# One 128-partition load with a zero-stride source in place of two 64-partition loads, in an attention block with two feed-forward layers

## What is computed

```python
h = _layernorm(x, axis=-1) * (1 + ca) + sa
q = (h @ Wq) -> (b, 16, l, 64);  k, v = (h @ Wk), (h @ Wv) -> (b, 4, l, 64), repeated 4 times
q = q * cos + _rotate_half(q) * sin        # k too
attn = einsum('bhqd,bhkd->bhqk', q, k) / 8 + slopes * rel
out = einsum('bhqk,bhkd->bhqd', softmax(attn), v) @ Wo
x = x + ga * out
```

## Time and profile before

| | us |
|---|---|
| median of 3 runs | 1219.91 (1217.07 to 1220.34) |
| profiled execution | 1218.02 |
| its span, first to last instruction | 1216.2 |
| PE / DVE / POOL / ACT busy | 1091.9 / 902.6 / 685.9 / 638.2 |
| DMA | 89.02 MB, mean 73 GB/s |
| stage one | 0 to about 120 |
| 32 heads | about 120 to 740 |

### The profile page before, as it was taken

The page is one execution under the profiler, slowest core; times in us unless marked ns, Lnnn a source line. Parts: engine busy times, 40 slices in busy tenths (PEclk is TensorE's granted clock), DMA queues, the critical chain, the costliest instruction groups (busy, mean ns, idle before and its releaser), DMA issues. The chain is left out here.

```text
span 1216.2 us, 23070 instructions
## 1 busy us (share of the span) xinstructions
PE 1091.9 (90%) x8352; PEld 666.1 (55%) x8352; DVE 902.6 (74%) x1584; ACT 638.2 (52%) x1000; POOL 685.9 (56%) x478
## 2 busy tenths in 40 slices
PE   5873799999999999999999999578899898999988
PEld 3552354554455545454544547446566795666678
DVE  6984776777777777777677744699998589888767
ACT  2442265656656665556565652145555555555554
POOL 3662156666667566665666665475555337555516
PEclk9996699999999999999999999789999999999999
DMA  8799412514325143152421100201111100111111
GB/s 245 252 246 341 103 39 59 113 37 100 72 49 114 38 107 71 41 114 50 101 71 36 45 19 26 72 18 29 31 24 37 25 2 18 30 30 31 31 26 34
DMA packets 83455, 89.02 MB, mean 73 GB/s; under 512 B 32740, under 2 KB 66064, under 8 KB 83344
## 3 DMA queue, kind: packets, MB, share of 16 engines
q1 hardware_dynamic: 83344, 87.55, 28.5%
HBM read 53.57 MB, written 24.25 MB: 64 GB/s over the span
## 5 line engine op out<-in xcount | busy, mean ns | idle before, releaser
L823 DVE CUSTOM_DVE_ANT_0 junk<-psum,alibi 128x1024 bf16<-128x1024 f32 x256 | 312.9, 1222 | 165.6 <-PE psum L888 158.3
L795 ACT ACTIVATE E<-psum,keybias_sb 128x1024 f32<-128x1024 f32 x256 | 274.8, 1112 | 190.2 <-PE psum L912 176.9
L732 POOL TENSOR_TENSOR xpos_sb<-xpos_sb,E 128x1024 f32<-128x1024 f32 x96 | 231.1, 2408 | 138.7 <-ACT E L795 134.3
L924 PE MATMUL psum<-E,V 128*64 128x512 f32 x1024 | 247.9, 605 | 0.0
L888 PE MATMUL psum<-KH,QH 64*128 64x512 f32 x512 | 121.2, 469 | 25.2 <-DVE M L823 20.0
L924 PEld LDWEIGHTS psum<-E,V 128*64 128x64 f32 x1024 | 62.1, 136 | 117.7 <-issue 111.7
L888 PEld LDWEIGHTS psum<-KH,QH 64*128 64x128 f32 x512 | 49.7, 190 | 119.2 <-DVE M L823 104.5
L736 POOL TENSOR_TENSOR xpos_sb<-xpos_sb 128x1024 f32<-128x1024 f32 x32 | 76.0, 2375 | 69.0 <-DVE xpos_sb L833 69.0
L912 PE MATMUL psum<-QH,KH 64*128 64x512 f32 x512 | 102.4, 396 | 0.7 <-DVE M L823 0.7
L912 PE MATMUL psum<-QL,KH 64*128 64x512 f32 x512 | 101.6, 392 | 0.0
L912 PE MATMUL psum<-QH,KL 64*128 64x512 f32 x512 | 101.5, 392 | 0.0
(11 more groups left out here) (145 smaller groups left out, 2143.8 us busy)
## 6 DMA issues: line engine op xcount, KB each, us to landing
QH<-qa_scratch SPq DMA_DIRECT2D x64, 256.0 KB, 4.7
qa_scratch<-tH SPq DMA_DIRECT2D x8, 1024.0 KB, 5.1
qa_scratch<-tL SPq DMA_DIRECT2D x8, 1024.0 KB, 7.4
QL<-qa_scratch SPq DMA_DIRECT2D x64, 128.0 KB, 4.8
XF<-inverse_scratch SPq DMA_DIRECT2D x32, 256.0 KB, 3.5
vp_att<-v_att SPq DMA_DIRECT2D x64, 128.0 KB, 2.3
KH<-k_scratch SPq DMA_DIRECT2D x16, 256.0 KB, 3.9
KL<-k_scratch SPq DMA_DIRECT2D x16, 256.0 KB, 5.1
```

The lines of the kernel that those rows point to most:

```text
L732: pool.tensor_tensor(sum_p[:, s, :], first, E[:, k % 4, :], ALU.add)\
L795: act.activation(E[:, k % 4, :], scores(k % 2), ACT.Exp, bias=kb).then_inc(exp_done, 1)
L823: dve.tensor_tensor_reduce(junk[:, :], banks(max_bank(i, k), 2), alibi[:, s, :], -1.0, BIG, ALU.add, ALU.min, M[:, s, k:k + 1]).then_inc(m ...
L924: last = pe.matmul(banks(6 + i % 2)[HD * ch:HD * ch + HD, :], V[:, g, k, :], E[:, k % 4, ch * 512:(ch + 1) * 512], start=(k == 0), stop=(k ...
```

## The change

The two transfers that fill the two halves of a tile become one over 128 partitions. Its source pattern has a leading dimension of 2: with stride zero for `QH`, `KH`, `KL` (the same 64 rows twice), with a stride of half a row for `QL`. The transfers of `V` stay. The counts that PE waits for follow: two transfers for queries instead of four, three for keys and values instead of five.

```diff
+        def twice(rows):
+
+            return rows[None].to_broadcast([2, HD, TB, P])
+
         def load_qa(sp, i, s):
             high, low = parts_of(qa_d, i // H, i % H)
-            for ch in range(2):
-                rows, half = slice(HD * ch, HD * ch + HD), slice(TB // 2 * ch, TB // 2 * (ch + 1))
-                sp.dma_start(QH[rows, s, :].bitcast(F32).rearrange("p (t c) -> p t c", c=P), high)\
-                    .then_inc(ld_qa[s], 16)
-                sp.dma_start(QL[rows, s, :].bitcast(F32).rearrange("p (t c) -> p t c", c=P), low[:, half])\
-                    .then_inc(ld_qa[s], 16)
+            sp.dma_start(QH[:, s, :].bitcast(F32), twice(high)).then_inc(ld_qa[s], 16)
+            sp.dma_start(QL[:, s, :].bitcast(F32), low.rearrange("p (a t) c -> a p (t c)", a=2)).then_inc(ld_qa[s], 16)
 
         def load_kv(sp, g, s):
             high, low = parts_of(k_d, g // KV, g % KV)
-            for dst, src in ((KH[0:HD], high), (KH[HD:P], high), (KL[0:HD], low), (KL[HD:P], low)):
-                sp.dma_start(dst[:, s, :].bitcast(F32).rearrange("p (t c) -> p t c", c=P), src)\
-                    .then_inc(ld_kv[s], 16)
+            for dst, src in ((KH, high), (KL, low)):
+                sp.dma_start(dst[:, s, :].bitcast(F32), twice(src)).then_inc(ld_kv[s], 16)
             sp.dma_start(V[:, s, :, :], v_d[g // KV, :, :, g % KV * HD:(g % KV + 1) * HD]).then_inc(ld_kv[s], 16)
...
-                            need(pe, ld_qa[s], 64 * (i // 4 + 1))
+                            need(pe, ld_qa[s], 32 * (i // 4 + 1))
                             if i % GROUP == 0:
-                                need(pe, ld_kv[g], 80 * (i // (2 * GROUP) + 1))
+                                need(pe, ld_kv[g], 48 * (i // (2 * GROUP) + 1))
```

## The result

The kernel with the change takes **1502.12 us** (median of 6 runs, 1498.96 to 1503.41) against 1219.54 (6 runs, 1217.07 to 1220.34): a ratio of 1.232 with an interval of 1.2301 to 1.2337. The profiled execution took 1502.15, its span is 1500.4. The forecast was 1445 with a range of 1400 to 1640: the sign and the mechanism are the forecast's, the time is 57 us above it. In the changed kernel the lines from L165 on are one lower than before (L912 is L911, L839 is L838), and the queries' loads are L164 and L165.

The account below looks back on a forecast made before the run. PE bounds the attention heads, DMA the first stage's loads and stores. Terms of +47.3 (first stage), +148.8 (groups), +12.7 (head 0), +2.4 (other heads) and +16 (clock) sum to 227 on 1218: 1445 us, range 1400 to 1640.

Parts of the forecast that it names:

- Two engines: Each merged load, its source led by 2, runs on two of 16 DMA engines, always the same two; chance 0.84.
- Rival 1: Merged loads use all 16 engines and both halves: up to 8.5 us faster, 1209.5 us; chance 0.08.
- rival 2: Merged loads use all 16 engines at today's rate: no change, 1218 to 1220 us; chance 0.03.
- rival 3: Merged loads run on two engines at 14.0 GB/s each: 2004 us; chance 0.05.
- QH's time to landing: Sign on the queries' load: its landing time rises from 4.7 to about 11 us or more.
- The price of a byte: Each of the two engines moves 26.9 GB/s, so a head's QH and QL take 14.6 us.
- First stage: Loads of three heads and one group take 63.3 us plus 1.0 for V instead of 17: +47.3 us.
- There is no cover left: In the first stage pair 4's stores queue behind the loads; ACT, DVE and PE, already 15.59 us late, wait for them.
- Ordinary heads: Heads without a new group turn from PE-bound to just DMA-bound: 19.2 us against 18.6, +0.6 each.
- closed loop: In heads, QH's issue through QM, den, reciprocal, inverse store and XF to the next QH: 19.2 us.
- Heads with a group: Heads loading new keys and values take 41.6 us; each of six groups costs +24.8 us, together +148.8.
- Clock: After PE idles in group heads, restarts run partly at 1.2 GHz: 2 to 3 us each, seven times, +16 us.

Follow-up runs that it names:

- leading 16: The changed kernel with its 128-partition loads read by a source pattern of 16 times 8 rows instead of 2 times 64: 1216.74 us, ratio 0.9994 to the kernel before.
- the kernel with keys alone: The kernel before with only the KH and KL loads merged, the queries in the old form: 1345.38 us, ratio 1.1046.

## Why the prediction was right, and where it was short

**Two engines (right, and this decides).** "Equal parts of both sides along the leading dimensions can only be two parts" held: shares of 0.12 to 0.16 for a count of 2, 0.26 for 4, full for 16, and the same path for a stride that is not zero. Rival 1 (one transfer over 128 partitions is fast) and rival 2 fell with these shares; rival 3 with the rate, 25 and not 14.0 GB/s. One sign that I named, QH's time to landing, could not be read: the page after has none for these loads. The transfers of the two busy engines also show which share comes late: of the eight packets of QM's two transfers in an ordinary head, four are out at 348.6 and 349.2, soon after their issue, and the other four start at 356.3, behind QL's last at 356.2.

**The price of a byte (mis-sized a little, for a reason that did not hold).** I took 26.9 GB/s per engine because I laid today's 14.0 to writing one half of the partitions at a time. The runs with both halves in flight and with leading 16 speak against the halves as the place where engines crowd. That two engines would not crowd held, so the choice was right on a reason that was half wrong. The packets of 4096 B took 162 ns (25.3 GB/s), those of 2048 B in QL 87 ns (23.5). QH and QL of a head are thus 10.4 + 5.6 = 16.0 us and not 14.6, and the three heads and one group of the first stage are 1.25 MB at 25.3 and 384 KB at 23.5: 51.8 + 16.7 = 68.5 instead of 63.3.

**First stage, forecast +47.3, measured +51.4.** By the rates just given it would be 52.5. "There is no cover left" proved true, as ACT's wait of 67.0 is 51.4 more than 15.6 was. The stage's very end is SP's last issue, as the runs with moved loads show, and in the changed kernel too:

```profile
169.82 1.47 SPq L328 DMA_DIRECT2D k_scratch<-tL  x1
...
172.22 1.22 PE L887 MATMUL psum<-KH,QH 64*128 64x512 f32 x4 [5.23 <-PEq L270]
```

That issue ends at 171.29, 0.93 before the first product. But the last four issues take 3.8 us (167.50 to 171.29), as in the kernel before, so nothing held them: here the release that I named, ACT's wait, carries the whole delay.

**Ordinary heads, forecast 19.2 and +0.6, measured 22.05 and +3.45.** This is the step that failed most, and its closed loop was right in kind: SP waits for the reciprocal, this for den, den for the bytes ahead of it on the two engines. From QH's issue to the reciprocal it is 19.86 us (337.99 to 357.85) where my terms gave 16.9. The rate explains 1.4. The packets in the trace place most of the other 1.5 behind the data: the last packet of QL starts at 356.22 and the last of den ends at 356.43, but the reciprocal starts at 357.85, 1.42 us later, where I had put 0.3 for den to land. I had taken den's 1.7 less 1.4 for its start, as if a transfer whose packets have moved had all but landed. The last 0.3 is in the start: 356.3 less 16.0 of data is 340.3, about 2.3 us after QH's issue instead of 2.0. A loop priced at 0.6 us above PE's time had to be priced closely: each error in it counts in full, three times per group.

**Heads with a group, forecast 41.6, measured 44.10.** Slower bytes add 1.2 for KH and KL and 1.4 for the queries, the late landing of den about 1.0 (here only the remainder of the sum); the wait of SP for the last product was shorter by 1.0 than the row that I took it from (1.45 from XF to KH, not 2.46). PE's wait in such a head is 25.25 us, where I had named some 22 as the sign. Group: 44.10 + 3 x 22.05 = 110.2, seen 109.9, forecast 99.2. Six times 10.7 is 64 us; the largest part of it is again the step above, three times in each group. With 4.1 of the first stage and 4.2 of the other heads (19.3 seen, 15.1 forecast), less the 16 of the next point, that is all but 1 of the 57 us by which the forecast was short.

**Clock, forecast +16, no such cost seen.** The clock did fall to 1.2 GHz in each hole (0.50 from 317 to 335.8), and PE's busy time rose by 34.9 us. But the loop of transfers sets the pace, and in the window 336 to 358, with a clock of 0.93, PE still had 1.57 us to spare. A slower restart inside a DMA-bound loop cost nothing that shows here; I counted it as if PE were the bound again. Where PE is the bound again after each hole, in the kernel with keys alone, a cost of this size is seen: the score products take 109.7 us more than before, and PE's waits for QM are 97.8 of it. This leaves 11.9 us, 1.7 for each of seven holes, while PE's busy time is 15.9 us longer. How much of that is the clock was not separated.

**The range** held because its slow end assumed a rate 20% lower. That was partly the wrong reason for the right width: the rate was 6 to 13% lower, and latencies in the loop did the rest, while the clock term, which was not paid, hid 16 us of the shortfall.

## What to carry to other kernels

Look at the leading dimension of both sides of a DMA, not at its partition count: a repeat or a split that puts a 2 in front left two engines to carry it, with a stride of zero and with one of half a row. A DMA share that sits near k/16 in a load stretch, with k the leading count, is how this shows. Then look at what small transfers stand behind it on those engines; here QM and den, a few KB each, were waited for 207.3 us by PE and 239.5 us by DVE. When a stage seems to wait for a landing, check also when the engine that issues the DMAs gets its last issue out, because the issue itself can be what ends last.

## What the runs showed of the hardware that I had not expected

- Sixteen engines are not enough for full rate. From 76 to 84 they moved 223 GB/s with a leading 16, and 331 with both sides led by 128. Eight engines ran at about 14 GB/s each, two or four at 24 to 25.
- Two halves from two queues were hardly faster than from one, 236 against 224 GB/s, with packets of both in flight together.
- One issue held SP for up to 11.06 us behind transfers on two engines. While QM's two issues took 8.41 us (from 318.15), the DMA share was 0.12 (317 to 335.8): 14 nearly free engines do not keep the queue moving.
- After den's last packet had moved it took another 1.42 us until the reciprocal could start: for a few KB this is far more than the packets' own time, and the loop pays it once in every head.
